# Attention and a recurrent block on one core: layer norms applied by ScalarE, the group norm's root by GpSimd, the loop written out, a new order of steps

## What is computed

```python
# block 0: attention over ctx (its own 32 heads of 16, keys and values of 8), then a layer norm
q, k, v = x @ Wq + bq, ctx @ Wk + bk, ctx @ Wv + bv
x = norm(softmax(q k / 4 + mask) v @ Wo + bo + x) * gamma + beta             # ln0
# block 1: recurrent mixing
xn = norm(x) * ln1_w + ln1_b                                                 # ln1
sx = shift(xn) - xn
x5 = xn + sx * (maa_stack + tanh((xn + sx * maa_x) @ maa_w1) @ maa_w2)       # five mixes
w = exp(-exp(time_decay + tanh(x5[1] @ decay_w1) @ decay_w2))
r, k, v, g = x5[3] @ Wr.T, x5[0] @ Wk.T, x5[2] @ Wv.T, silu(x5[4] @ Wg.T)
for t in tokens:                                # per head, a 16 x 16 state s
    out[t] = r[t] . (u * k[t] v[t]' + s);  s = k[t] v[t]' + w[t] * s
x = x + (groupnorm(out) * g) @ Wo.T             # mean and variance of 16 values
xn2 = norm(x) * ln2_w + ln2_b                                                # ln2
x = x + sigmoid(mix_r @ ffn_Wr.T) * (relu(mix_k @ ffn_Wk.T)**2 @ ffn_Wv.T)
```

## Time and profile before

| | |
|---|---|
| median of 3 runs | 2512.75 us (2511.68 to 2516.52) |
| the profiled execution | 2511.9 us, of it 2510.1 us from the first to the last instruction (the span) |
| TensorE busy, matmuls | 2306.4 us, 92% |
| VectorE busy | 2164.8 us, 86% |
| ScalarE busy | 942.2 us, 38% |
| GpSimd busy | 568.3 us, 23% |
| mean granted TensorE clock | 0.958 of 2.4 GHz |

### The profile page before, as it was taken

One profiled execution on the slowest core, in us unless ns is written; L12 is line 12 of the kernel. 1 busy time (PEld: TensorE's weight loads), 2 busy tenths in 40 slices (PEclk: granted clock), 3 DMA queues, 4 the chain that ended last, 5 costly groups with the idle time before them and its releaser, 6 DMA issues. The chain is left out here.

```text
span 2510.1 us, 43786 instructions
## 1 busy us (share of the span) xinstructions
PE 2306.4 (92%) x14144; PEld 1578.5 (63%) x14144; DVE 2164.8 (86%) x5337; ACT 942.2 (38%) x3169; POOL 568.3 (23%) x762
## 2 busy tenths in 40 slices
PE   4697999999999999999999999999999999999966
PEld 3474766667576675757657575665757666675633
DVE  1368999999989898998989889898898999999993
ACT  2434352624425252442624335262342526244111
POOL 1122223131222313122131212213122231322200
PEclk8798999999999999999999999999999999999977
DMA  7000001010000101001010100101001010100000
GB/s 249 19 10 29 1 10 37 2 46 1 19 29 10 38 1 46 1 10 38 10 37 1 39 9 10 38 10 37 1 14 34 10 37 4 44 1 20 8 17 9
DMA packets 48435, 61.86 MB, mean 25 GB/s; under 512 B 20208, under 2 KB 25968, under 8 KB 48208
## 3 DMA queue, kind: packets, MB, share of 16 engines
q1 hardware_dynamic: 48208, 58.93, 7.5%
HBM read 42.14 MB, written 16.78 MB: 23 GB/s over the span
## 5 line engine op out<-in xcount | busy, mean ns | idle before, releaser
L1140 DVE TENSOR_TENSOR_SCAN st<-ws,st 128x256 f32<-128x256 f32 x1024 | 620.5, 671 | 10.5 <-POOL st L994 10.4
L851 ACT ACTIVATE probs_or_mixes<-probs_or_mixes,least 128x128 f32<-128x128 f32 x1024 | 396.8, 397 | 25.1 <-DVE least L1087 24.6
L1150 DVE TENSOR_TENSOR st<-st,rT 128x1024 f32<-128x1024 f32 x256 | 327.5, 1280 | 19.4 <-issue 16.6
L1129 DVE TENSOR_TENSOR st<-bank_pair,kT 128x1016 f32<-128x1016 f32 x256 | 309.8, 1210 | 37.1 <-PE bank_pair L701 36.3
L1087 DVE CUSTOM_DVE_ANT_0 probs_or_mixes<-bank,nmask 128x128 f32<-128x128 f32 x1024 | 228.8, 285 | 55.8 <-PE bank L569 34.1
L1018 POOL TENSOR_TENSOR probs_or_mixes<-probs_or_mixes 128x512 f32<-128x512 f32 x160 | 187.4, 1193 | 268.0 <-DVE probs_or_mixes L1212 268.0
L1024 POOL TENSOR_TENSOR rstd<-rstd,mhalf 128x1 f32<-128x1 f32 x96 | 80.1, 835 | 701.4 <-DVE rstd L1169 701.4
L701 PE MATMUL bank_pair<-v_hi,sel 32*128 32x256 f32 x1024 | 187.3, 346 | 50.1 <-DVE st L1129 50.0
L994 POOL COPY st<-s 128x8 f32<-128x8 f32 x256 | 76.5, 312 | 646.3 <-PE bank L724 423.9
L851 ACT ACTIVATION_READ_ACCUMULATOR probs_or_mixes<-probs_or_mixes,least 128x1 f32 x1024 | 201.0, 196 | 0.0
L701 PEld LDWEIGHTS bank_pair<-v_hi,sel 32*128 32x128 f32 x1024 | 110.2, 189 | 131.3 <-DVE st L1129 70.9
(11 more groups left out here) (137 smaller groups left out, 4210.4 us busy)
## 6 DMA issues: line engine op xcount, KB each, us to landing
cin<-in_ctx SPq DMA_DIRECT2D x16, 512.0 KB, 3.7
xin<-in_x SPq DMA_DIRECT2D x16, 512.0 KB, 3.7
x<-xin SPq DMA_DIRECT2D x16, 512.0 KB, 3.7
keep<-x SPq DMA_DIRECT2D x16, 512.0 KB, 3.9
out<-keep SPq DMA_DIRECT2D x32, 256.0 KB, 2.0
wo<-in_wo SPq DMA_DIRECT2D x2, 1024.0 KB, 11.4
nmask<-in_mask SPq DMA_DIRECT2D x16, 128.0 KB, 4.5
wq<-in_wq SPq DMA_DIRECT2D x1, 1024.0 KB, 9.5
```

Source lines behind the costliest of these rows:

```text
L851: last = fn(pr[:, n % 4, j, :], pr[:, n % 4, j, :], ACT.Exp, bias=least[:, n, j:j + 1], scale=-1.0, accum_out=rsum[:, n, j:j + 1])
L1129: tt(dst, src, over(kv, DU, 1), ALU.mult).then_inc(outer.sem, 1)
L1140: last = nc.vector.tensor_tensor_scan(v, ws[:, c].rearrange("p b t -> p (b t)"), v, 0.0, ALU.mult, ALU.add)
L1150: tt(v, v, over(rT[:, u // PER, :], DU, 1), ALU.mult).then_inc(weighed.sem, 1)
```

## The change

- The six applied layer norms of a group move from VectorE to ScalarE, as one activation each, `x * root + (-mean * root)`. `statistics` on VectorE also writes minus the mean to a new column `less`; GpSimd multiplies it by the root behind the power.
- Newton's method goes. A new step `power.0` on GpSimd raises variance + eps, 128 x 256, to the power -0.5 in one instruction; TensorE's `rstd` steps wait for it.
- The copies that stood behind `apply1.1` and `apply2.1` become steps `row1` and `row2` of VectorE's own.
- The loops go: all 18 iterations are written out, on all engines and on SP.
- All four orders are new. The order of transfers on SP stays.

```diff
 PE_ORDER = """
+mean.0+2 turn_c.0 proj_k.0+1 decay.0+1 proj_v.0+1 proj_r.0+1 decay.1+1 turn_x.0 turn_c.1 spread.0+1 turn_x.1
+reduce.6+2 reduce.7+2 key.0 mean.1+2 query.0 spread.1+1 low_rank.4+1 score.0 query.1 var.0+2 spread.2+1 proj_r.1+1
+score.2 spread.3+1 proj_g.0+1 rstd.0+2 rstd.1+2 proj_g.1+1 turn_p.0 spread.4+1 score.4 reduce.0+1 turn_p.1 out.0+2
...
 ACT_ORDER = """
...
+key.0 mean.1+2 query.0 query.1 score.0 proj_r.1+1 score.1 proj_g.0+1 score.2 score.3 proj_g.1+1 turn_p.0 turn_p.1
+turn_p.2 apply2.0+2 turn_p.3 score.4 score.5 score.6 turn_p.4 score.7 turn_p.5 turn_p.6 score.8 proj_v.1+1 turn_p.7
+turn_p.8 flip.0 score.9 score.10 proj_k.1+1 score.11 apply2.1+2 share.0 turn_p.9 score.12 turn_p.10 turn_m.0+2
+turn_p.11 score.13 turn_m.1+2 turn_p.12 score.14 score.15 turn_p.13 turn_p.14 turn_p.15 flip.1 apply0.0 share.1
+ffn_k.0+2 apply0.1 ffn_r.0+2 apply1.0 ffn_k.1+2 apply1.1 ffn_r.1+2 turn_n.0 turn_n.1
 POOL_ORDER = """
...
+rk.0+1 turn_x.0 first.2+1 negate.0 mix.4+1 first.3+1 power.0+2 first.4+1 turn_x.1 norm2.0+2 first.5+1 rk.1+1
...
 DVE_ORDER = """
+scan.0+1 mix.4+1 outer.1+1 weigh.0+1 score.0 scan.1+1 score.1 outer.2+1 var.0+2 weigh.1+1 score.2 keep_row.0+1
+outer.3+1 scan.2+1 score.3 groupnorm.0+2 proj_g.0+1 scan.3+1 weigh.2+1 proj_g.1+1 score.4 row2.0+2 weigh.3+1
+outer.4+1 score.5 scan.4+1 out.0+2 key.0 value.0 norm2.0+2 weigh.4+1 score.6 outer.5+1 score.7 out.1+2 scan.5+1
...
+inverse.1 norm0.0 scan.8+1 gather.1 weigh.8+1 readout.1+1 norm1.0 project.1 norm0.1 row1.0 scan.9+1 outer.10+1
...
-            for it in range(LOOP_FROM):
-                once(it)
-            with eng.Fori(LOOP_FROM, LOOP_TO) as i:
-                once(i)
-            for it in range(LOOP_TO, G + LATEST):
+            for it in range(G + LATEST):
                 once(it)
...
+            def apply(n, src, dst):
+                def step(g, b):
+                    if n == 2 and b == 0 and known(g + C_AHEAD):
+                        act.wait_ge(filled[XB.of(("turn_c", 1))], XB.through(("turn_c", 1), g + C_AHEAD))
+                    act.wait_ge(pw_n[n].sem, pw_n[n].after(g, b + 1))
+                    fn(dst[:, b, :], src[:, b, :], ACT.Identity, bias=less[:, n, b:b + 1],
+                       scale=rstd[:, n, b:b + 1]).then_inc(ap_n[n].sem, 1)
+                return step
...
-                    tt(v, v, mhalf[:, 0:1], ALU.pow).then_inc(pw_n[n].sem, 1)
+                    tt(v, v, mhalf[:, 0:1], ALU.pow).then_inc(ro_n[n].sem, 1)
+                    pool.wait_ge(ro_n[n].sem, ro_n[n].after(g, b + 1))
+                    m = less[:, n, b:b + 1]
+                    tt(m, m, v, ALU.mult).then_inc(pw_n[n].sem, 1)
...
+            def power(g, _):
+                hold(pool, emptied, g, through("var", 0))
+                tt(y, vs, mhalf[:, 0:1].to_broadcast([P, T]), ALU.pow).then_inc(rooted.sem, 1)
...
+                wait(dve, ap_n[n].sem, ap_n[n].after(g - 1, b + 1))
+                ts(less[:, n, b:b + 1], aggr[:, n, b, 0:1], -1.0, None, ALU.mult)
                 ts(rstd[:, n, b:b + 1], aggr[:, n, b, 1:2], eps, None, ALU.add).then_inc(rs_n[n].sem, 1)
```

More of the change, by code:

```diff
@@ new lines @@
+reduce.6+2 reduce.7+2 key.0 mean.1+2 query.0 spread.1+1 low_rank.4+1 score.0 query.1 var.0+2 spread.2+1 proj_r.1+1
+score.2 spread.3+1 proj_g.0+1 rstd.0+2 rstd.1+2 proj_g.1+1 turn_p.0 spread.4+1 score.4 reduce.0+1 turn_p.1 out.0+2
+turn_p.2 value.0 turn_p.3 spread.5+1 score.6 out.1+2 reduce.1+1 values.0 turn_p.4 spread.6+1 score.8 turn_p.5
+turn_p.6 proj_v.1+1 turn_p.7 score.10 values.1 spread.7+1 turn_p.8 flip.0 proj_k.1+1 spread.8+1 score.12 turn_p.9
+share.0 reduce.2+1 turn_m.0+2 turn_p.10 score.14 spread.9+1 turn_p.11 turn_m.1+2 turn_p.12 values.2 project.0
@@ L130 @@
+turn_p.13 turn_p.14 reduce.3+1 turn_p.15 spread.10+1 flip.1 values.3 share.1 ffn_k.0+2 project.1 ffn_k.1+2 ffn_r.0+2
+spread.11+1 ffn_r.1+2 turn_n.0 turn_n.1 reduce.4+1 spread.12+1 ffn_v.0+2 low.0 ffn_v.1+2 spread.13+1 low_rank.0
+reduce.5+1 low_rank.2 spread.14+1 tdecay.0 spread.15+1
 """
 ACT_ORDER = """
-turn_c.0 turn_x.0 turn_c.1 decay.0+1 proj_v.0+1 turn_x.1 proj_r.0+1 decay.1+1 mean.1+2 proj_r.1+1 query.0 key.0
-proj_g.0+1 proj_v.1+1 score.0 score.1 score.2 proj_g.1+1 query.1 turn_p.0 turn_p.1 score.3 turn_p.2 score.4 turn_p.3
@@ L135 @@
[L135 to L138, removed]
+low.0+1 tdecay.0+1 turn_c.0 mean.0+2 decay.0+1 proj_k.0+1 proj_v.0+1 proj_r.0+1 turn_x.0 turn_c.1 decay.1+1 turn_x.1
+key.0 mean.1+2 query.0 query.1 score.0 proj_r.1+1 score.1 proj_g.0+1 score.2 score.3 proj_g.1+1 turn_p.0 turn_p.1
@@ L143 @@
-norm2.1+2 turn_x.1 rk.2+1 first.7+1 norm0.0 first.8+1 first.9+1 affine0.0 norm1.0 norm0.1 affine0.1 rk.3+1 first.10+1
-norm1.1 first.11+1 first.12+1 mix.0 first.13+1 mix.1 mix.2 first.14+1 first.15+1 mix.3 first.0
+affine0.1+1 norm1.1+1 first.12+2 mix.0+1 mix.1+1 first.13+2 first.14+2 first.15+2 mix.2+1 mix.3+1 first.0+1 first.1+1
+rk.0+1 turn_x.0 first.2+1 negate.0 mix.4+1 first.3+1 power.0+2 first.4+1 turn_x.1 norm2.0+2 first.5+1 rk.1+1
+first.6+1 first.7+1 norm2.1+2 first.8+1 first.9+1 rk.2+1 first.10+1 norm0.0 affine0.0 rk.3+1 norm1.0 first.11+1
@@ L145 @@
+norm0.1
 """
 DVE_ORDER = """
[L148 to L156, removed]
+scan.0+1 mix.4+1 outer.1+1 weigh.0+1 score.0 scan.1+1 score.1 outer.2+1 var.0+2 weigh.1+1 score.2 keep_row.0+1
@@ new lines @@
+outer.3+1 scan.2+1 score.3 groupnorm.0+2 proj_g.0+1 scan.3+1 weigh.2+1 proj_g.1+1 score.4 row2.0+2 weigh.3+1
+outer.4+1 score.5 scan.4+1 out.0+2 key.0 value.0 norm2.0+2 weigh.4+1 score.6 outer.5+1 score.7 out.1+2 scan.5+1
+score.8 score.9 readout.0+1 weigh.5+1 outer.6+1 norm2.1+2 inverse.0 proj_v.1+1 score.10 scan.6+1 outer.7+1 score.11
+scan.7+1 score.12 score.13 gather.0 outer.8+1 weigh.6+1 score.14 weigh.7+1 score.15 outer.9+1 shift2.0+2 project.0
+inverse.1 norm0.0 scan.8+1 gather.1 weigh.8+1 readout.1+1 norm1.0 project.1 norm0.1 row1.0 scan.9+1 outer.10+1
@@ L157 @@
+weigh.9+1 norm1.1 outer.11+1 scan.10+1 weigh.10+1 shift.0 outer.12+1 scan.11+1 weigh.11+1 scan.12+1 ffn_v.0+2
+ffn_v.1+2 mix.0 mix.1 outer.13+1 mix.2 outer.14+1 readout.2+1 mix.3 outer.15+1 scan.13+1 scan.14+1 weigh.12+1
+scan.15+1 weigh.13+1 proj_v.0 weigh.14+1 weigh.15+1 outer.0 readout.3+1
 """
@@ L171 @@
 LATEST = max(late for t in (PE_STEPS, ACT_STEPS, POOL_STEPS, DVE_STEPS) for _, _, late in t)
-LOOP_FROM, LOOP_TO = 2 * LATEST, G - LATEST
-C_AHEAD = next(late for name, n, late in DVE_STEPS if name == "apply2")
+C_AHEAD = next(late for name, n, late in ACT_STEPS if name == "apply2")
 RING, READOUT = [0, 1, 2, 4], 7
@@ L309, in build @@
         rs_n = [Signal(sem(f"ln{n}_var_eps"), NB) for n in range(3)]
+        ro_n = [Signal(sem(f"ln{n}_root"), NB) for n in range(3)]
         pw_n = [Signal(sem(f"ln{n}_rstd"), NB) for n in range(3)]
@@ L964, in _ @@
                 proj_v=evac_proj("proj_v", v_hi, v_free, v_rounded), proj_g=proj_g, mean=mean, turn_m=turn_m,
-                ffn_k=ffn_k, ffn_r=ffn_r))
+                ffn_k=ffn_k, ffn_r=ffn_r,
+                apply0=apply(0, xin, xin), apply1=apply(1, xin, lnb), apply2=apply(2, keep, ln2)))
         @block.gpsimd
@@ L1040, in _ @@
                 turn_x=turn_x, negate=negate, norm0=inverse_root(0), norm1=inverse_root(1),
-                norm2=inverse_root(2), affine0=affine0, mix=mix, first=first_state,
+                norm2=inverse_root(2), affine0=affine0, mix=mix, power=power, first=first_state,
                 rk=r_times_k))
@@ L1185, in norm1, with row1 @@
                 statistics(g, b, 1, xin, EPS)
[L1187 to L1191, removed]
+            def row1(g, _):
+                hold(dve, emptied, g, through("project", NB - 1))
+                dve.wait_ge(rows_saved.sem, rows_saved.after(g, 1))
+                nc.vector.tensor_copy(xnT[:, :, :, 0], prev[:, :, :, 1]).then_inc(rows_copied.sem, 1)
             def shift(g, _):
@@ L1279, in norm2, with row2 @@
                 statistics(g, b, 2, keep, EPS)
[L1281 to L1289, removed]
-                    nc.vector.tensor_copy(mnT[:, :, :, 0], src[:]).then_inc(rows2.sem, 1)
+            def row2(g, _):
+                dve.wait_ge(row_kept.sem, row_kept.after(g, 1))
+                wait(dve, row_moved.sem, row_moved.after(g + 1, 1) if known(g + 1) else 0)
+                hold(dve, filled, g, through("ffn_v", NB - 1, back=1))
+                src = prev3 if known(g + 1) else prev2
+                nc.vector.tensor_copy(mnT[:, :, :, 0], src[:]).then_inc(rows2.sem, 1)
             def shift2(g, _):
@@ L1326, in _ @@
                 key=key, value=value, score=score, inverse=inverse, gather=gather, project=project, outer=outer_, scan=scan,
-                weigh=weigh, readout=readout, norm0=norm0, apply0=apply0,
-                norm1=norm1, apply1=apply1, norm2=norm2, apply2=apply2, shift=shift, mix=mix, keep_row=keep_row,
+                weigh=weigh, readout=readout, norm0=norm0, row1=row1, row2=row2,
+                norm1=norm1, norm2=norm2, shift=shift, mix=mix, keep_row=keep_row,
```

29 lines of the change are left out of this document (4 added, 25 removed).

## The result

The changed kernel takes 3071.35 us (median of 4 runs, 3062.08 to 3072.98) against 2513.19 before, a ratio of 1.221 with a 95% interval from 1.218 to 1.224. 2443 was forecast, with a range from 2405 to 2477: the forecast is wrong, on the wrong side. What happened is rival (c), which had 0.13 of the chances, at a length of the power of 42 us.

A forecast was written before the change was run, and what follows sets the result against it. TensorE and VectorE were taken to pace each other, TensorE a little ahead. 2511.9 - 49.3 (loop turns) - 21 (shorter periods) + 0.5 (ends) = 2442, and 2443 for the median, 0.9 above; range 2405 to 2477.

The forecast's parts named there:

- rival (c): GpSimd's power outlasts its 7 us of cover and TensorE waits in each group: 2764 at 27 us; chance 0.13.
- the price of the power: Group norm's root as one GpSimd power over 256 columns, shown by no row: taken as 6 us, between 0.73 and 69.
- the 0.27: Microseconds by which a one-column GpSimd power (0.552 us) was taken to exceed a one-column product (0.28 us).
- The upper bound of 69 us: Longest power on GpSimd, if all the extra 0.27 us of one column came back in each of 256 columns.
- The 2.6 us estimated beside the sum: GpSimd's power over 256 columns, estimated from the skill's some 12 cycles an element at 1.2 GHz.
- rival (b): Short power on GpSimd and TensorE nearly gapless: 2411 us; chance 0.15.
- The cover: TensorE's work between var.0 and rstd.0, 10.4 us, less delays before the power starts: 7.0 us to hide it.
- The lock: VectorE and GpSimd hold each other out for whole instructions: power 1.22 us late, keep_row's copies waiting some 5 us.
- The 5 us of VectorE that I charged: VectorE's keep_row copies waiting for the power's end, some 5 us where one lost 1.0 before; net relief -2.9 us a period.
- The turns: Nine loop turns at 5.5 us on TensorE, issue gap and slow matmuls behind it: 49.3 us saved by straight code.
- the relief with the new order: Less VectorE work and new orders remove 1.5 of TensorE's 4.5 idle us a period: 21 us over fourteen periods.
- the head and the end: Bare norm chains grow (+2.2 and +2.4 us), VectorE-bound iterations shrink: net +0.5 us, between -5 and +6.

The follow-up runs named there:

- 16 columns: The changed kernel with GpSimd's power over only 16 of its 256 columns, the rest set to 1 (for timing only): 2445.45 us, ratio 0.972.

## Why the prediction was wrong

**The step that failed** is the price of the power: "since the 0.27 also holds what is set up once, I take 6". The 0.27 us by which a one-column power was taken to be dearer than a one-column product were 0.36 (0.552 less the 0.194 that such a product takes in the new kernel), and 0.16 of them come back in every column: 256 x 0.159 + 0.37 = 41.1 us. The upper bound of 69 us held it; the choice inside the bounds didn't. A middle on a scale of ratios is no estimate, and the argument for going below it had no row behind it. The one in rival (c), that a wide program overlaps its columns as the product does, was false too. The 2.6 us estimated beside the sum, which spoke for rival (b), was a sixteenth of what was measured; the measurement decides.

**The cover** was 4.8 us, or 3.9 without the 0.92 for weigh.1, as the prediction counts; 7.0 had been worked out. TensorE's way from var.0 to rstd.0 was right, 10.1 against 10.4. But VectorE reads the variance 4.86 us behind L735, not 1.57: scan.1 and score.1 also stand ahead of it, and outer.2 starts only at 1576.38. In the old order, where the 1.57 had been read, the cover was 7.3 us. So rival (c)'s mechanism was right and its sum short: 37.3 x 16 = 597 instead of (42 - 7) x 15 = 525, and it had left out the lower clock: of the 3071.35 - 2445.45 = 626 us between 256 and 16 columns the wait is 596 (600.0 less 3.6 in the last group of the latter), and some 30 are left for it.

**The lock** didn't show behind the power. Weigh.1 held it up by 0.92 us, where 1.22 was forecast (the one-column power of the earlier trace rows ends at 1992.38, 0.41 us behind its weigh, not with it). But keep_row's copies took 0.16 and 0.17 us under it and four scans 2.43, their usual time. The 5 us of VectorE that I charged weren't there.

**What was right.** The turns: 49.3 us forecast, 49.1 measured (2513.19 - 2464.05). VectorE's busy time fell from 135.2 us a period to between 128.2 and 129.1, that is by 6.1 to 7.0 (6.9). GpSimd's small product takes 0.194 us (0.28), ScalarE's apply 0.81 (0.63 by the square, which has no scale and bias columns). And the relief with the new order: 2464.05 - 2445.45 = 18.6 us against 21. TensorE's idle time in a period fell from 4.3 to 2.9 us, by 1.4 where 1.5 was forecast; its busy time fell by 0.8 as well, which nobody had forecast. With its power covered, the kernel takes 2445 where I said 2443. That this is so near is partly luck. The thirteen full periods went from (2154.74 - 286.06) / 13 = 143.7 us in the written-out kernel to (2146.86 - 305.34) / 13 = 141.7 with 16 columns, where 142.2 was forecast; that is 27 us, and the head and the end took 8.6 us longer where 0.5 was forecast.

**Whose the relief is.** In the old order neither part shortens the full period of 143.7: it is 143.5 with Newton's work gone (the whole kernel is 5.6 us shorter, little more than the noise between two sets of runs) and 143.9 with the applies moved. The new order with both has 141.7. Both in the old order at once, and the new order without the moved applies but with a covered power, weren't run, so the two can't be told apart further. With Newton kept and the applies moved, the new order takes 2530.58 us, 61 more than the old one with the same work (2469.31), so it is no gain by itself.

**The chances.** Rival (c) had 0.13, though the only row on the power allowed anything up to 69 us and everything over 10 meant a loss. On a scale of ratios from 0.73 to 69 about 0.4 lies above 10.3. The unknown price should have set the chances, and the range.

**What follows for the kernel.** The fastest here that computes all of the reference is the kernel before with its loops written out, 2464.05 us. Covering a 42 us power by a later rstd wasn't tried: `proj_g` of the next group overwrites `gT`, and waits for groupnorm.

## What to carry to other kernels

An operation that no row shows, at a width that no row shows, decides everything if someone waits for it: price it by its linear worst case, or give the chances by how much of the span between its bounds lies beyond the break-even point. Newton's eleven cheap instructions on VectorE, 4.7 us, beat one instruction of 42 us on an idle engine. Where an iteration stands both written out and in a loop in one trace, the difference of the periods is the loop's price: 49.3 us by it, 49 to 51 measured. And an order fitted to one set of durations has no room for others: look for the stretch in which an engine shows no gap, since its share over the period hides it.

## What the runs showed of the hardware

- GpSimd's power costs 0.159 us a column for 128 partitions, linear from 16 to 256 columns, beside 1.8 ns for a product.
- A GpSimd instruction that waits for VectorE and one that holds it out aren't the same. The power started 0.16 us behind weigh.1 and took 0.92 us longer than alone, but under the rest of its 41 us the copies took 0.16 and 0.17 us and four scans 2.43, while the gamma product of the earlier trace rows made such a copy take 1.18. In the old order, where the scans start with the power, four took 2.89. The Trainium skill (SBUF — State Buffer, Who interferes with whom) has the first to start exclude the other for its whole length, for a VectorE instruction in a two-port mode or with two inputs from SBUF; the copies, and the scans with their two inputs from SBUF, don't agree with it. Why the power lets them pass, no run shows.
- A turn of a loop cost 4.7 to 5.5 us on TensorE: a gap of 2.1 to 4.6 us, mostly 3, and the clock's lower level behind it.
- TensorE's clock after a gap: 3.57 us of idle time ahead of proj_g.1 was followed by a granted clock of 0.55 and 6.69 us for what takes 3.72 at the 2.4 GHz level.
